# A recurrence step whose hidden-part fold reads three PSUM banks instead of interleaved SBUF rows

## What is computed

```python
xw = jnp.einsum('ntd,dh->nth', x, Wx) + b       # N=8 sequences, T=128 steps, D=H=128
def step(prev_h, xw_t):
    next_h = jnp.tanh(xw_t + prev_h @ Wh)
    return (next_h, next_h)
_, hs = jax.lax.scan(step, h0, jnp.swapaxes(xw, 0, 1))
...
x = x + attention(hs)                            # and the later stages
```

## Time and profile before

| | us |
|---|---|
| median of 3 runs | 3063.25 (3061.85 to 3064.69) |
| profiled execution, its own time | 3067.32 |
| its span on the core | 3065.5 |
| recurrence | about 13 to 1911 of the span |
| attention and layers | the rest |

### The profile page before, as it was taken

The page is one execution under the profiler, slowest core; times in us unless marked ns, Lnnn a source line. Parts: engine busy times, 40 slices in busy tenths (PEclk is TensorE's granted clock), DMA queues, the critical chain, the costliest instruction groups (busy, mean ns, idle before and its releaser), DMA issues.

```text
span 3065.5 us, 51933 instructions
## 1 busy us (share of the span) xinstructions
PE 2581.4 (84%) x12402; PEld 1508.3 (49%) x12465; DVE 2690.4 (88%) x7345; ACT 2261.6 (74%) x4810; POOL 2368.9 (77%) x2545
## 2 busy tenths in 40 slices
PE   4878888887888888888878887876999999999997
PEld 2334433343433343333434333663666666667665
DVE  3999999999999999999999998656999999999996
ACT  3777777777777777777777776335888888888886
POOL 5777777777777777777777777007999999999994
PEclk9999999999999999999999999898999999999998
DMA  5333343333333333333333334200001010101000
GB/s 133 75 71 75 69 76 72 72 71 75 76 69 75 71 75 69 76 75 70 71 74 75 69 76 73 77 1 1 1 3 36 0 40 0 40 0 40 0 0 8
DMA packets 368014, 163.08 MB, mean 53 GB/s; under 512 B 285158, under 2 KB 298220, under 8 KB 367212
## 3 DMA queue, kind: packets, MB, share of 16 engines
q1 hardware_dynamic: 367980, 162.65, 25.7%
HBM read 156.81 MB, written 5.80 MB: 53 GB/s over the span
## 4 chain that ended last, share of the span: by engine, by line
DVE 33%; PE 22%; issue 20%; POOL 15%; ACT 6%; DMA 1%; POOLq 1%; SPq 1%; DVEq 0%; ACTq 0%
PE bank L1487 9%; POOL qk L714 8%; PE bank L1551 6%; DVE bank L1114 4%; PE bank L1502 4%; DVE bank L1109 3%; ACT qkv_w L798 3%; DVE sq L1089 3%; DVE bank L1089 3%; POOL rs L723 3%; DVE fix_trace L1180 3%; POOL qk L729 2%; ACT qkv_w L821 2%; DVE sq L1172 2%; DVE qkv_w L1114 1%
## 5 line engine op out<-in xcount | busy, mean ns | idle before, releaser
L628 POOL TENSOR_TENSOR kT<-upto,xT 128x512 f32<-128x512 f32 x260 | 270.1, 1039 | 380.8 <-PE bank L1492 380.8
L1114 DVE TENSOR_REDUCE bank<-qkv_w 128x2 f32<-128x768 f32 x512 | 466.1, 956 | 89.0 <-ACT qkv_w L821 74.1
L1487 PE MATMUL bank<-diag_h,w_part 128*128 128x512 f32 x1024 | 374.9, 488 | 161.5 <-DVE bank L1109 161.5
L1114 DVE TENSOR_REDUCE qkv_w<-qkv_w 128x4 f32<-128x1536 f32 x256 | 447.9, 1750 | 49.9 <-ACT qkv_w L814 32.7
L814 ACT COPY qkv_w<-bank 128x512 f32<-128x512 f32 x258 | 220.8, 856 | 255.3 <-PE bank L1487 255.3
L1487 PE MATMUL bank<-diag_x,w_part 128*128 128x512 f32 x1032 | 386.9, 496 | 13.4 <-DMA diag_x<-diag_ring 13.4
L642 POOL TENSOR_TENSOR diag_h<-eye,part 128x512 fp32r<-128x512 f32 x384 | 388.5, 1040 | 0.0
L1487 PEld LDWEIGHTS bank<-diag_h,w_part 128*128 128x128 f32 x1024 | 184.5, 190 | 410.4 <-issue 386.5
L1502 PE MATMUL bank<-qT,wh 128*128 128x256 f32 (+1 forms) x768 | 255.4, 468 | 149.8 <-DVE qT L1096 148.5
L723 POOL TENSOR_TENSOR rs<-rs,halfs 128x8 f32<-128x8 f32 x192 | 368.3, 1918 | 16.0
L1724 PE MATMUL bank<-qkv_w,xsT 128*128 (+1 forms) x576 | 308.6, 619 | 10.3 <-DVE rot_s L1336 8.0
(11 more groups left out here) (238 smaller groups left out, 6550.5 us busy)
## 6 DMA issues: line engine op xcount, KB each, us to landing
diag_x<-diag_ring SPq DMA_DIRECT2D x259, 512.0 KB, 7.2
qkv_w<-in_L_ffn_Wqkv SPq DMA_DIRECT2D x6, 1536.0 KB
diag_ring<-X SPq DMA_DIRECT2D x264, 4.0 KB, 5.6
diag_ring<-o_fin SPq DMA_DIRECT2D x8, 512.0 KB, 7.8
o_w<-in_L_ffn_Wo SPq DMA_DIRECT2D x6, 512.0 KB
w<-in_L_ffn_W SPq DMA_DIRECT2D x6, 341.0 KB
b<-in_L_ffn_b SPq DMA_DIRECT2D x6, 341.0 KB
w<-in_L_ffn_W SPq DMA_DIRECT2D x6, 128.0 KB
```

The lines of the kernel that those rows point to most:

```text
L628: pool.tensor_tensor(tri[n][:, rows, :], upto[:].unsqueeze(1).to_broadcast([P, 4, D]), src[:, rows].unsqueeze(2).to_broadcast([P, 4, D]), ...
L1114: return dve.tensor_reduce((pre, bias_at[0])[n][:, a:b], chain[n][:, a:b, :], AX_X, ALU.add)
L1487: return pe.matmul(dst, w_part[:, n, w], diag[n][:, d, a:b, :].rearrange("p n k -> p (n k)"), start=False, stop=True, skip_group_check=True)
```

## The change

The three links of h are left in PSUM, one bank for each: rests in banks 0 and 3, guesses in 1 and 4, minus the guesses in 2 and 5 (first and second half). The fold of a half of h is one reduction over three banks and 128 positions. ACT copies the guesses of h to SBUF contiguously (`guess_h`), for the difference on DVE and the identity matmul on PE; the rests of h are no longer copied. The offset is taken off the guesses on PE, by one more one-row bf16 matmul for each half (`less_offset_h`). Minus the guesses is written by ACT for both halves (`place_minus_h`), and POOL no longer does that. A fold of x writes its result (with the bias, the start of h's chain) to the last place of the minus bank. `SUM_BANKS_X` is still `REST_BANKS_H`, so the guesses of x now wait for the folds of h (`h_folded`) rather than for copies of rests. On ACT, two of the four `lower_h` diagonals come before the second copy and two after `place_minus_h(0)`. The three reductions at the end of the program are gone. The tiling of x, `tanh()`, all other stages and all loops are as before.

```diff
-REST_BANKS_H, REST_BANKS_X = (2, 3), (4, 6)
+REST_BANKS_H, GUESS_BANKS_H, MINUS_BANKS_H = (0, 3), (1, 4), (2, 5)
 SUM_BANKS_X = REST_BANKS_H
-OWN_BANKS = (5, 7)
+REST_BANKS_X = MINUS_BANKS_H
+OWN_BANKS = (6, 7)
...
+        guess_h = qkv_w[:, 0, 0:NB * D].rearrange("p (n k) -> p n k", n=NB)
+        minus_h = [bank_rows(which) for which in MINUS_BANKS_H]
+        links_h = [bank[:, first:first + 3, :].rearrange("p c (n k) -> p n k c", k=D) for first in REST_BANKS_H]
...
# POOL, in the loop
-                minus_h(counts[0])
...
# ACT
+            def copy_guess_h(half, count):
 
                 act.wait_ge(sum_ready[0], count)
-                act.activation(adds[0][:, 4 * half:4 * half + 4, :, 1], bank[:, half, :].rearrange("p (n k) -> p n k", k=D),
-                               ACT.Identity, bias=offset[:, 0:1], scale=1.0).then_inc(guess_placed, 1)
+                act.copy(guess_h[:, 4 * half:4 * half + 4, :], bank_rows(GUESS_BANKS_H[half])).then_inc(guess_copied, 1)
...
+            def place_minus_h(half):
+
+                act.activation(minus_h[half][:, :, 0:D - 1], bank_rows(GUESS_BANKS_H[half])[:, :, 0:D - 1], ACT.Copy,
+                               scale=-1.0).then_inc(minus_placed[half], 1)
...
                 triangle_mid()
-                act.wait_ge(less_guess, counts[1])
-                place_guess_h(0, counts[0])
-                place_guess_h(1, counts[1])
+                copy_guess_h(0, counts[0])
+                act.wait_ge(split_h, this)
+                lower_h(4)
+                copy_guess_h(1, counts[1])
+                act.wait_ge(rest_placed_x, counts[1])
                 less_guess_of_h()
-                act.wait_ge(split_h, this)
-                lower_h()
-                place_rests_h(0, counts[0])
-                place_minus_h()
-                place_rests_h(1, counts[1])
+                act.wait_ge(diff_ready, this)
+                act.wait_ge(x_folded, this)
+                place_minus_h(0)
+                lower_h(6)
+                act.wait_ge(x_scanned, this)
+                place_minus_h(1)
...
# DVE
+                if not isinstance(this, int):
+                    dve.wait_ge(h_ready, value(dve, this - 1))
                 dve.tensor_copy(h_now[:], h_own).then_inc(h_static, 1)
...
+                dve.wait_ge(guess_copied, count)
+                dve.tensor_scalar(dst[:, :, 0:1], guess_h[:, rows, 0:1], -1.0, None, ALU.mult)
+                dve.tensor_tensor(dst[:, :, 1:], bank_rows(GUESS_BANKS_H[half])[:, :, 0:D - 1], guess_h[:, rows, 1:],
+                                  ALU.subtract).then_inc(diff_ready, 1)
+
+            def fold_x(half):
+                rows = slice(4 * half, 4 * half + 4)
+                return dve.tensor_reduce(minus_h[half][:, :, D - 1], chain[:, rows, :], AX_X, ALU.add)
+
+            def fold_h(half):
+                return dve.tensor_reduce(pre[:, 4 * half:4 * half + 4], links_h[half], mybir.AxisListType.XY, ALU.add)
...
                     placed_x(counts[0])
-                    n_x = step(fold(1, 0, 4))
+                    fold_x(0).then_inc(x_folded, 1)
                     difference_h(0, counts[0])
                     placed_x(counts[1])
-                    fold(1, 4, 8).then_inc(x_scanned, 1)
-                    after(n_x)
-                    for m in range(4):
-                        placed_h(m)
-                        if m == 2:
-                            dve.wait_ge(x_scanned, this)
-                        n_h = step(fold(0, 2 * m, 2 * m + 2))
-                    after(n_h)
+                    fold_x(1).then_inc(x_scanned, 1)
+                    for half, done in ((0, x_folded), (1, x_scanned)):
+                        dve.wait_ge(done, this)
+                        dve.wait_ge(rest_ready[0], counts[half])
+                        dve.wait_ge(minus_placed[half], this)
+                        fold_h(half).then_inc(h_folded, 1)
+                    dve.wait_ge(h_folded, counts[1])
                     tanh()
...
-            dve.tensor_reduce(small[:, 0:2], bank[0:SN, 0:3, 0:2 * D].rearrange("p c (n k) -> p n k c", k=D),
-                              mybir.AxisListType.XY, ALU.add)
...
# PE, in the loop
                 pe.wait_ge(tri_h_mid, this)
-                sums_h(0, 2, 4).then_inc(sum_ready[0], 1)
+                sums_h(0, 2, 4)
+                less_offset_h(0).then_inc(sum_ready[0], 1)
                 pe.wait_ge(tri_h_second, this)
-                sums_h(1, 4, 8).then_inc(sum_ready[0], 1)
+                sums_h(1, 4, 8)
+                less_offset_h(1).then_inc(sum_ready[0], 1)
...
-                        pe.matmul(bank[:, REST_BANKS_H[1], :].rearrange("p (n k) -> p n k", k=D)[:, :, 1:], eye[:],
-                                  adds[0][:, 4:8, 0:D - 1, 1], start=False, stop=True, skip_group_check=True)
+                        pe.matmul(bank_rows(REST_BANKS_H[1])[:, :, 1:], eye[:], guess_h[:, 4:8, 0:D - 1], start=False,
+                                  stop=True, skip_group_check=True)
...
                 for half in range(2):
-                    pe.wait_ge(rest_placed[0], quarters[half])
+                    pe.wait_ge(h_folded, counts[half])
                     sums_x(half, counts[2 + half])
...
-                pe.wait_ge(minus_placed[1], this)
                 offset_h()
```

More of the change, by code:

```diff
@@ L278, in program, with bank_rows @@
         minus_eye = qk[:, 2, 0:P]
-        adds = [qkv_w[:, n, :].rearrange("p (n i c) -> p n i c", n=NB, c=3) for n in range(2)]
-        bias_at = [tile[:, :, D - 1, 2] for tile in adds]
-        chain = [qkv_w[:, n, :].rearrange("p (n i) -> p n i", n=NB) for n in range(2)]
+        adds = qkv_w[:, 1, :].rearrange("p (n i c) -> p n i c", n=NB, c=3)
+        bias_at = adds[:, :, D - 1, 2]
+        chain = qkv_w[:, 1, :].rearrange("p (n i) -> p n i", n=NB)
+        guess_h = qkv_w[:, 0, 0:NB * D].rearrange("p (n k) -> p n k", n=NB)
+        def bank_rows(which):
+            return bank[:, which, :].rearrange("p (n k) -> p n k", k=D)
+        minus_h = [bank_rows(which) for which in MINUS_BANKS_H]
+        links_h = [bank[:, first:first + 3, :].rearrange("p c (n k) -> p n k c", k=D) for first in REST_BANKS_H]
         ring = nc.dram_tensor('diag_ring', (RING, P, 2, NB, D), F32, kind='Internal').ap()
@@ L634, in place_sums_x @@
                 pool.wait_ge(guessed, count)
[L635 removed]
+                pool.tensor_tensor(adds[:, rows, :, 1], src,
                                    offset[:, 0:1].unsqueeze(2).to_broadcast([P, 4, D]), ALU.add)
[L637 to L638 removed]
+                pool.tensor_scalar(adds[:, rows, 0:D - 1, 2], src[:, :, 0:D - 1], -1.0, OFFSET, ALU.mult, ALU.add).then_inc(
+                    sum_placed_x, 1)
             def diagonal(n, d, half, values, done):
@@ L773, in _, with lower_h @@
             act.activation(bpc[:], bank[:, 3, 0:1], ACT.Identity, bias=bp[:], scale=1.0).then_inc(bpc_ready, 1)
-            def lower_h():
-                for n in range(4, 8):
+            def lower_h(first):
+                for n in (first, first + 1):
                     ins = act.activation(diag[0][:, 1, n, :], eye[:], ACT.Copy, scale=part[:, 1, n:n + 1])
@@ L1495, in offset_h, with less_offset_h @@
             def offset_h():
-                for half in range(2):
-                    pe.matmul(bank[:, half, :], offset16[:, 0:D], offset16[:, D:], start=True, stop=True,
+                for which in GUESS_BANKS_H:
+                    pe.matmul(bank[:, which, :], offset16[:, 0:D], offset16[:, 2 * D:], start=True, stop=True,
                               skip_group_check=True)
+            def less_offset_h(half):
+                return pe.matmul(bank[:, GUESS_BANKS_H[half], :], offset16[:, D:2 * D], offset16[:, 2 * D:], start=False,
+                                 stop=True, skip_group_check=True)
             def sums_h(half, a, b):
-                return pe.matmul(bank[:, half, (a - 4 * half) * D:(b - 4 * half) * D], wh[:],
+                return pe.matmul(bank[:, GUESS_BANKS_H[half], (a - 4 * half) * D:(b - 4 * half) * D], wh[:],
                                  tri[0][:, a:b, :].rearrange("p n k -> p (n k)"), start=False, stop=True,
@@ L1536, in _ @@
                 landed = value(pe, 16 * t + 32)
-                quarters = [value(pe, 4 * t + n) for n in (2, 4)]
                 pe.wait_ge(tri_h_first, this)
```

76 lines of the change are left out of this document (24 added, 52 removed).

## The result

The changed kernel takes **3090.73 us** (median of 15 runs, 3069.24 to 3101.37), the kernel before 3063.42 (15 runs, 3060.85 to 3067.69). The ratio is 1.0086 [1.0071, 1.0101]: it is slower by 27 us, where 17 us less were forecast. The profiled execution took 3091.48, its span is 3089.3.

A forecast was written before the change was run, and what follows sets the result against it. No engine is full; a chain of waits between engines sets 14.53 us a step. 0.12 saved over 126 steps (15.1), plus 2.7 at the end, less 1.15, gives -16.6: median 3046.6 us, range 3028 to 3075.

The forecast's parts named there:

- The new waits: Walk from the last fold of h through guesses of x, POOL, second guesses, ACT and both folds: 14.41 us a step.
- What would show it: Signs listed for the trace: step of 14.4, PE's second guesses waiting for POOL, folds of h at 1.75.
- the slower one: Rival: PSUM traffic disturbs folds of h, 1.87 each, 0.24 a step more; 14.65 a step, 3077 us; chance 0.18.
- last diagonals, exit: Recurrence's end: attention waits for the last diagonals' DMA, behind later rests of x; 1.15 us lost once.
- end of the program: The three reductions at the program's end go, straight on the path; 2.7 us saved.
- The path: Longest circle from last fold to last fold, through PE, POOL, PE, ACT and DVE; 14.41 us a step.
- a surcharge on PSUM: Rival: folds on PSUM cost their own overhead, 0.13 more a step; loop gains nothing, 3062 us; chance 0.14.
- disturbed folds: Rival: PE and ACT writing neighbouring banks slow folds of h to 1.87 each; 3077 us; chance 0.18.
- The loop turn of DVE: Every fourth step, 0.5 us of issue ahead of the first fold of x; now hidden by DVE's wait for the guesses' copy.
- the circle through the rests: From `less_guess` through identity matmul and rests on PE, ending 12.55; second fold of h starts 12.66; hardly shorter.
- The circle through ACT and DVE: Rests of x, placing, guesses, copy, difference, second fold of x: DVE free at about 10.9, 0.1 ahead of minus the guesses.
- the guesses of x behind the folds: Second half's guesses wait for the last fold; POOL 1.5 us late, giving back nearly all of over a microsecond.

The follow-up runs named there:

- experiment 1: Changed kernel plus one unread full-height bf16 matmul on PE between the first `less_offset_h` and the wait for POOL's triangle; 3029.15 us, ratio 0.9888.
- experiment 2: Changed kernel with the offset matmuls over 128 rows, 127 of them zero, instead of one row; 3018.55 us, ratio 0.9849.
- experiments 4: Kernel before with one wait added: the second half's guesses of x wait for the last fold of h; 3252.73 us (one run).
- experiment 7: experiment 2 with the guesses of x written to banks 0 and 1, so both wait only for the first fold of h; 2947.31 us, ratio 0.9615.
- experiment 5: Changed kernel plus one 128-row matmul behind the first half's guesses of x, ahead of PE's wait for the last fold; 3159.64 and 3281.78 us.

## Why the prediction was wrong

**The step that failed is one that isn't written in it:** every duration of PE was taken from rows at full clock, and nothing allowed for the clock of the new order. The low clock stands in the sum at nothing; it measured 58.7 us. The part "The new waits" put PE's second guesses behind POOL, and "What would show it" names that wait; the one-row matmul ahead of it stands in the sum at 0.31. Both were right, and together they are the place where the clock falls. None of the rivals was about the clock; the slower one was priced by PSUM traffic under the folds, and was wrong.

The ledger from before to after, in us of the profiled spans (3065.5 to 3089.3, +23.8):

| | forecast | measured |
|---|---|---|
| 126 steps at full clock | -15.1 (14.53 to 14.41) | -30.3 (14.53 to 14.29) |
| low clock in the recurrence | 0 | +58.7 |
| start-up, to the third copy of h | 0 | -2.9 (80.29 to 77.44) |
| last diagonals, exit | +1.15 | +0.8 (4.75 to 5.54) |
| end of the program | -2.7 | -2.6 |

The last line is what is left of the part behind the last copy of h, 1.8 shorter in all. Without the 58.7 the kernel would be at 3090.7 - 58.7 = 3032.0; experiment 1, which gives the clock back and nothing else, measured 3029.

The Trainium skill tells of such falls, and I had not weighed it: "TensorE: Matmul & The Clock Gate", section "A second HAM failure mode: psum-queue depth-cycling", describes another kernel in which PE "micro-idles between MM groups frequently enough" that its clock goes back and forth between the two levels. The trace agrees so far: 34 falls, with no wait of PE over 0.6 us in a clean step. By the section "HAM oscillation — how this bites in real kernels" of this page of the Trainium skill the loss is half of the time at the lower clock, an estimate of 157 x 0.5 = 78 us. Measured are 58.7; part of the longer work fills waits that PE has in a clean step anyhow (6.60 us busy in the 6.60 from 982.60 on). Part 3 of the same page of the Trainium skill, "Packing small matmuls — row/col tiling", says that a matmul with few rows leaves most of the array idle. No trace shows the array; what goes with the height in this case is what experiment 2 shows, no fall instead of 34.

**The path was right.** Walked from the end E of the last fold, in us:

| | forecast | measured |
|---|---|---|
| guesses of x done | 1.22 | 1.25 (714.12 to 714.25 + 1.12) |
| POOL's triangle of x starts | 1.40 | 1.44 |
| POOL's triangle of h starts, ends | 6.54, 7.58 | 6.60, 7.64 |
| second guesses and their offset done | 9.11 | 9.13 |
| minus the guesses, ACT | 10.96 | 10.73 |
| end of both folds | 14.41 | 14.29 |

(For the lower rows E is that of the step before, 714.12 - 14.29 = 699.83.) The one mis-sized term is ACT's: I added 0.59, 0.57 and 0.65; the three follow each other after 0.49 and 0.51, and the last takes 0.56, 1.56 in all. DVE then starts 0.13 behind ACT instead of 0.04. That is the 0.12 of a step. The folds were forecast at 3.41 for both and take 3.43; so the rivals of a surcharge on PSUM and of disturbed folds fall. By the overheads that the prediction takes from the Trainium skill ("Perfetto Trace Analysis", section "Optimizing Scalar/DVE Operations") a fold from PSUM would take 65 ns more than one from SBUF, as an estimate. Measured are 6 (1762 against 1756), and the measurement decides. The loop turn of DVE is absorbed, as forecast: the clean steps don't differ by four. That the circle through the rests is hardly shorter was right: they end at 12.41 by E (712.24), and the second fold starts at 12.54 (712.37), so neither end alone could have bought much. The circle through ACT and DVE was forecast to leave DVE free at about 10.9; it measures 10.40 (708.48 + 1.75 less 699.83), so it was further off the limit than thought.

**The cost of the wait.** The prediction says that the guesses of x behind the folds give back nearly all of the gain. The direction is shown by experiments 4 and 7: the wait costs 1.1 us a step in the kernel before, and 0.57 where experiment 7 undoes it. The size was too large: from 14.53 to 13.62 the gain would be 0.91 a step, and of this the wait returns 0.57, well over half and not nearly all. That the wait costs less in the changed kernel may be because the change shortens the same circle elsewhere; this is argued, not shown.

## What to carry to other kernels

When a change splits PE's stretches by waits, even of 0.2 to 0.4 us, and puts matmuls of few rows between them, write down for each stretch what PE does ahead of its next long matmul and keep a rival in which the clock falls there: here it turned a gain of some 31 us into a loss of 27. The cure was cheap here: give such a matmul all 128 rows (zeros), or put a matmul of full height at that place; one at another place did harm. And if a buffer is freed by the last of several operations, look for one that the first of them frees: that was worth 71 us more.

## What the runs showed of the hardware that I had not expected

- The granted clock in a recurrence fell 34 times in 126 steps, with PE busy 90% of the span and no wait of it over 0.6 us in a clean step. With PE's one-row matmuls at full height, or one wait of 0.37 less, it fell not once in the 126 steps.
- It is not idle time alone. The kernel before waits longer in each step (PE's timeline of before, below), and its clock never fell in the 126 steps. What the chip counts was not settled.

```profile
1010.89 1.99 PE L1502 MATMUL bank<-qT,wh 128*128 128x256 f32 x6 [1.17 <-DVE qT L1096]
1014.10 1.20 PE L1487 MATMUL bank<-diag_h,w_part 128*128 128x512 f32 x4 [1.22 <-DVE bank L1109]
```

- Long falls come in rows of slowed steps (17.07 us each), in after up to 6, in experiment 5 rows of 4, 8, 3 and 26. The times of one kernel spread with the clock: in after 3069 us at a mean of 0.970 and 3101 at 0.958, in experiment 5 3160 at 0.935 and 3282 at 0.893. What starts and ends such a row was not settled.
- A change of height from 128 rows to one or back cost PE 0.1 to 0.2 us of overlap in the steps compared; experiment 2's step is 0.10 shorter.
- A reduction over three PSUM banks runs as fast as one over SBUF: 1762 against 1756 ns for 1,536 elements.
- Copies of 512 elements from PSUM on ACT issue every 0.49 to 0.51 us, although each one takes 0.56 to 0.59.
